# Four-bit feed-forward with its norm inside the rounding stage, and a sign layer joined with its norm

## The chip, the cores and the metric

The kernel runs on one core of a Trainium2 chip. The metric is the device time of one execution in microseconds (us). The engines are TensorE (PE, matmuls; PEld its weight loads), VectorE (DVE), ScalarE (ACT), GpSimd (POOL) and SyncE (SP, which issues DMAs here). Each works through its own instructions in order and waits at semaphores for the others. Data lies in SBUF or in PSUM, the memory that TensorE writes.

## The reference, cut to what matters

A stream of 8 sequences of 512 tokens with 128 channels passes eight layers, each added to the stream after a layer norm (state space, four-bit feed-forward, linear attention, four-bit feed-forward, forgetting attention, sign layer, rotary attention, sign layer). The two layers that the change rewrites:

```python
def _layernorm(x, axis=-1, eps=1e-05):
    m = jnp.mean(x, axis=axis, keepdims=True)
    v = jnp.var(x, axis=axis, keepdims=True)
    return (x - m) / jnp.sqrt(v + eps)
def fp4_quant_dequant(x):             # BLOCK = 16 along the last dimension
    xb = x.reshape(shape[:-1] + (shape[-1] // BLOCK, BLOCK))
    scale = jnp.max(jnp.abs(xb), axis=-1, keepdims=True) / 6.0
    scale = jnp.maximum(scale, jnp.float32(1e-12))
    xn = xb / scale
    idx = jnp.searchsorted(_MID, jnp.abs(xn))
    q = _GRID[idx] * jnp.sign(xn) * scale      # grid 0, .5, 1, 1.5, 2, 3, 4, 6
    return q.reshape(shape)
def _L0_ffn_ref(x, w_gate, w_up, w_down):      # 128 -> 352 -> 128
    gate = fp4_linear(x, w_gate)               # both sides are rounded first
    y = fp4_linear(x, w_up)
    h = jax.nn.silu(gate) * y
    return fp4_linear(h, w_down)
def _L1_ffn_ref(x, weight):
    return jnp.einsum('bsi,oi->bso', x, jnp.sign(weight))
...
x = x + _L0_ffn_ref(_layernorm(x, axis=-1), ...)
```

## The kernel before, in words

The stream `X` and its norm `XN` stay in SBUF as 128 channels x 8 sequences x 512 tokens in f32. The program is a row of stages. A `Stage` (L55) ends with a barrier of all engines, so nothing of one stage runs beside the next. Its tiles carry its name as a prefix in the trace (`ln_`, `fx_`, `fh_`, `sf_`, `fu_`). An f32 matmul shows as two PE instructions, a transpose as one.

`layernorm_stage` (L133) writes `XN`, a sequence at a time: TensorE subtracts the mean by a matmul with `center`, VectorE copies the result out (L208), ScalarE squares it, TensorE sums the squares of four sequences into one PSUM tile, ScalarE takes Ln and Exp, VectorE refines the inverse root by one Newton step of three operations (`refine`, L212 to L216), TensorE spreads it (L169) and VectorE multiplies (L221).

`ffn0_stages` (L647) has two stages. `fx` rounds the normed tokens, one sequence at a time. ScalarE copies, TensorE transposes to 128 tokens x 128 channels (L676), VectorE takes each block's largest magnitude, makes `scale` and a slightly larger `above`, divides, and finds a rounding constant `mag` for each value from its exponent bits by two operations. GpSimd adds and subtracts `mag`, which rounds. VectorE multiplies by `scale` (L720), and TensorE turns it back (L682). `fh` works on 32 tiles of 128 tokens. For each, TensorE multiplies by the gate and up weights (128x352, L767, L768), ScalarE takes Tanh, VectorE forms `h` in SBUF and rounds it as in `fx`, two tiles in step. GpSimd adds, subtracts and multiplies by `scale` (L861 to L868), TensorE transposes (L775), ScalarE copies to `HT`, and once per sequence (four tiles) TensorE multiplies by the down weights into `y` (L782) and VectorE adds that to `X` (L843). VectorE's nine operations stand in loops over tile pairs, of which each ends before the next:

```python
for t, done in both:
    dve.wait_ge(s.amax, done)
    dve.tensor_scalar(scale[t][:, :], amax[t][:, :], 1.0 / 6.0, 2e-12, ALU.mult, ALU.max).then_inc(s.scale, 1)
for t, done in both:
    dve.tensor_scalar(above[t][:, :], amax[t][:, :], ABOVE / 6.0, ABOVE * 2e-12, ALU.mult, ALU.max).then_inc(s.above, 1)
```

`ffn1_stage` (L964) multiplies `XN` by the signs of the weights (L976) and VectorE adds to `X` (L983). After the last one a stage of its own stores `X` by four DMAs (L248).

`forget_units` (L1059) is one pipeline over 64 units (a sequence and two heads). In its turns `i` from -8 a unit `a = i + 8` is projected (`kvps`, L1224), filtered by six VectorE operations in `KV` (L1425, `tap`), passed through Tanh back into `kvps` (L1304), and multiplied into keys and values (L1452, L1453). The projection of a unit waits for the values of the one before:

```python
pe.wait_ge(s.sk, a)
pe.wait_ge(s.sv, a)
```

The scores start at `i = 0`, so in the first turns only these steps run. `nps`, `sps` and `P13` serve the scores and are idle until then.

## Time and profile before

| what | value |
|---|---|
| median of 3 runs (lowest, highest) | 2548.9 us (2546.92, 2555.17) |
| profiled execution, its own time | 2549.09 us |
| its span | 2547.3 us |
| busy, PE / DVE / ACT / POOL | 1965.4 / 1695.2 / 1371.0 / 966.0 us |

The profile is one execution. The span runs from the first instruction to the last. Busy shares are means over stages that have different limits, so the profile is read stage by stage: the timeline gives where a stage begins and ends, and within it the engine that never idles, or the chain of waits, sets its length. The forgetting attention takes the largest part of the span (L1059 and on), and little of it is touched.

### The profile page before, as it was taken

What the parts mean: (1) busy time and instruction counts of PE and PEld (TensorE: products, weight loads), DVE (VectorE), ACT (ScalarE), POOL (GpSimd) and SP (SyncE); (2) the same over time, 40 slices, a digit from 0 to 9 for tenths busy, and PEclk for the clock granted to TensorE, in tenths of its full rate; (3) what the DMA queues carried; (4) which work ended last, traced back from release to release, by engine and by line L of the source; (5) the groups of instructions that cost most, each with busy time, mean ns of one, the idle gap of its engine ahead of it and who ended that gap; (6) DMA issues with size and microseconds to landing.
All of it is one profiled execution on the core that took longest, in us unless ns stands there. A gap on an engine that the chain in (4) does not pass through costs nothing. (4 is left out here: it accounts for less than half of the span.)

```text
span 2547.3 us, 38051 instructions
## 1 busy us (share of the span) xinstructions
PE 1965.4 (77%) x11759; PEld 874.1 (34%) x11759; DVE 1695.2 (67%) x2691; ACT 1371.0 (54%) x2091; POOL 966.0 (38%) x810
## 2 busy tenths in 40 slices
PE   5368876276782664589999999999999867589885
PEld 2123321133451331244444444444444313222221
DVE  5979985588435884577888888788886436611113
ACT  3356652122341222467777777777775513398882
POOL 0256661357003570144455555455555403600000
PEclk9779997578895886899999999999999968799998
DMA  2000000000000001011111111121111100411110
GB/s 84 0 13 0 0 0 0 0 0 0 0 0 0 1 0 48 22 42 53 56 56 60 54 54 54 60 64 59 54 63 61 40 15 25 100 43 44 49 37 33
DMA packets 66118, 85.81 MB, mean 34 GB/s; under 512 B 13344, under 2 KB 37216, under 8 KB 65888
## 3 DMA queue, kind: packets, MB, share of 16 engines
q1 hardware_dynamic: 60944, 81.37, 10.4%
q10 hardware_dynamic: 5040, 2.72, 0.4%
q8 instruction: 76, 1.25, 0.2%
q14 instruction: 58, 0.48, 0.1%
HBM read 72.12 MB, written 11.93 MB: 33 GB/s over the span
## 5 line engine op out<-in xcount | busy, mean ns | idle before, releaser
L1425 DVE SCALAR_TENSOR_TENSOR fu_kv<-fu_ps_kv,fa_vec,fu_kv 128x511 f32<-128x511 f32 (+2 forms) x384 | 265.4, 740 | 22.6 <-ACT fu_kv L1342 21.7
L1782 ACT ACTIVATE rt_p<-rt_ps_s 128x1024 f32<-128x1024 f32 x256 | 242.7, 1026 | 43.7 <-PE rt_ps_s L1719 43.0
L1497 POOL TENSOR_TENSOR fu_p<-fu_p 128x768 f32<-128x768 f32 x64 | 116.9, 1826 | 262.6 <-PE fu_ps_n L1196 258.2
L1166 PE MATMUL fu_ps_s<-fu_qn,fu_kn 64*128 64x512 f32 (+3 forms) x1024 | 191.2, 471 | 7.5 <-ACT fu_p L1329 5.6
L600 POOL TENSOR_TENSOR scan_hC<-scan_h,scan_c 128x1024 f32<-128x1024 f32 x64 | 150.8, 2356 | 83.0 <-DVE scan_h L580 83.0
L1224 PE MATMUL fu_ps_kv<-w_XN,fa_wp 128*128 128x512 f32 x256 | 138.3, 666 | 42.0 <-DVE fu_vs L1453 26.7
L1196 PE MATMUL fu_ps_n<-fu_p,fu_vt 128*64 128x512 f32 (+3 forms) x1024 | 166.0, 445 | 0.0
L525 PE MATMUL scan_ps_y<-scan_hC,w_ident 128*128 128x512 f32 x256 | 130.4, 633 | 41.0 <-POOL scan_hC L600 24.3
L580 DVE TENSOR_TENSOR_SCAN scan_h<-scan_dA,scan_ps_b 128x1024 f32<-128x1024 f32 x64 | 146.4, 2287 | 2.2
L1508 POOL TENSOR_TENSOR fu_num<-fu_num,fu_sg 128x512 f32<-128x512 f32 x64 | 81.4, 1272 | 168.9 <-DVE fu_sg L1458 168.9
L1730 PE MATMUL rt_ps_o<-rt_p,rt_va 128*32 128x512 f32 x1024 | 137.9, 611 | 4.5 <-POOL rt_va L1707 3.5
L1166 PEld LDWEIGHTS fu_ps_s<-fu_qn,fu_kn 64*128 64x128 f32 x1024 | 82.8, 185 | 126.7 <-ACT fu_p L1346 52.1
L1719 PE MATMUL rt_ps_s<-ra_stackq,ra_stackk 48*128 48x512 bf16 x512 | 92.7, 390 | 41.5 <-ACT rt_p L1782 22.6
L1342 ACT ACTIVATE fu_kv<-fu_ps_kv,fa_vec 128x512 f32<-128x512 f32 x128 | 86.6, 687 | 68.2 <-PE fu_ps_kv L1224 63.9
L1398 DVE SCALAR_TENSOR_TENSOR fu_og<-fu_num,fu_ow,fu_ro 128x512 f32<-128x512 f32 x64 | 81.0, 1266 | 57.6 <-POOL fu_num L1508 49.8
L1492 POOL TENSOR_TENSOR fu_kn<-fu_ks,fu_rb 128x512 f32<-128x512 f32 x64 | 98.7, 1543 | 40.2 <-DMA fu_rb<-rms_rows 40.1
L1402 DVE TENSOR_REDUCE fu_nm<-fu_ps_m 128x2 f32<-128x1024 f32 x64 | 78.0, 1219 | 45.2 <-PE fu_ps_m L1189 45.2
L561 ACT ACTIVATE scan_c<-scan_ps_c 128x1024 f32<-128x1024 f32 x64 | 65.5, 1024 | 75.6 <-POOL scan_hC L600 46.5
L796 ACT ACTIVATE fh_th<-fh_ps_g 128x352 f32<-128x352 f32 x64 | 29.7, 464 | 134.7 <-PE fh_ps_u L768 134.7
L1458 DVE SCALAR_TENSOR_TENSOR fu_sg<-fu_sg,fu_ps_s 128x512 f32<-128x512 f32 x64 | 44.0, 688 | 80.3 <-ACT fu_sg L1318 80.0
L1487 POOL TENSOR_TENSOR fu_sqk<-fu_ks 128x512 f32<-128x512 f32 x64 | 66.6, 1040 | 78.9 <-DVE fu_ks L1452 78.5
L1707 POOL COPY rt_va<-ra_v 128x128 f32 x32 | 8.1, 296 | 232.7 <-PE rt_ps_o L1730 232.3
(311 smaller groups left out, 5115.8 us busy)
## 6 DMA issues: line engine op xcount, KB each, us to landing
fu_rb<-rms_rows SPq DMA_DIRECT2D x256, 128.0 KB, 2.9
fu_ro<-rms_rows SPq DMA_DIRECT2D x128, 128.0 KB, 3.0
ra_stackq<-rope_parts SPq DMA_DIRECT2D x168, 32.0 KB
ra_stackk<-rope_parts SPq DMA_DIRECT2D x168, 32.0 KB
rope_parts<-rp_q SPq DMA_DIRECT2D x24, 128.0 KB, 2.0
rope_parts<-rp_k SPq DMA_DIRECT2D x24, 128.0 KB, 2.0
rms_rows<-fu_r SPq DMA_DIRECT2D x14, 192.0 KB, 2.1
w_X<-in_xT SPq DMA_DIRECT2D x4, 512.0 KB
```

The source lines that it names most:

```text
L525: i = pe.matmul(yps[:, :], w.ident[:, :], hC[p % (BEHIND + 2)][:, j, :], start=(p == 0 and j == 0), stop=(p == PAIRS - 1 and j == 1))
L580: dve.tensor_tensor_scan(flat[0], flat[1], flat[2], 0.0, ALU.mult, ALU.add).then_inc(s.scan, 1)
L600: pool.tensor_tensor(hC[p % (BEHIND + 2)][:, :, :], hst[p % 2][:, :, :], csb[p % 2][:, :, :], ALU.mult).then_inc(s.hC, 1)
L1166: pe.matmul(sps[:, h, at:at + T - t * P], k[head(h), t * P:(t + 1) * P], q[head(h), t * P:T], start=(at == 0), stop=False)
L1196: m = pe.matmul(nps[head(h), t * P:T], VT[b % VR][:, t, head(h)], p[:, h, :], start=(t == 0), stop=(t == 2))
L1224: pe.matmul(kvps[:, j, :], wp[:, g, 1 + j, :], XN[:, n, :], start=True, stop=True).then_inc(s.kvp, 1)
L1425: dve.scalar_tensor_tensor(acc, kvps[:, k, 0:T - j], vec[:, a % GA, at:at + 1], acc, ALU.mult, ALU.add).then_inc(done, 1)
L1492: pool.tensor_tensor(KN[u % 3][:, :], K[u % KR][:, :], RB[:, 1, :], ALU.mult).then_inc(s.kn, 1)
L1497: pool.tensor_tensor(tail, tail, P13[:, :, 0:3 * P], ALU.add).then_inc(s.d1, 1)
L1719: m = pe.matmul(sps[i][:, e, :], stack[1][rows, 2 * q4 + i, t * P:(t + 1) * P], stack[0][rows, 2 * q4 + i, :], start=True, stop=True)
L1730: m = pe.matmul(ops[q4 % 2][32 * j:32 * j + 32, :], va[:, t, 4 * q4 + j, :], pr[k % 2][j // 2][:, j % 2, :], start=(t == 0), stop=(t == NT ...
L1782: act.activation(pr[k % 2][i][:, :, :], sps[i][:, :, :], ACT.Exp, scale=DH_B ** -0.5).then_inc(s.exp, 1)
```

## The change: what it does

The stages `ln2`, `ln4`, `ln6` and `ln8` are gone.

**fx.** It works on pairs of sequences (four pairs, tiles of 128 tokens x 1024). TensorE makes the centred tokens at once in token rows (`center(k)`, with a piece of `X` as the stationary side) into a ring of three PSUM tiles. ScalarE squares with a sum per token (8 instructions of 128x128 a pair), and Ln and Exp of 128x8 give the rough inverse root. VectorE refines it on 128x8 tiles. It takes block maxima of the centred values, and one multiplication in place in PSUM applies norm and scale together. ScalarE takes absolute values times 2^22 (`size`), VectorE forms `tot` = max(`size`, ROUND) + value, GpSimd forms `mag` = max(`size`, ROUND), `q` = `tot` - `mag`, and multiplies by `above`. The multiplication that VectorE did at L720 is thus GpSimd's.

**fh.** The tiles run singly, with no loop instructions. `h` and the scaled value stay in PSUM (`ups`, three tiles). ScalarE takes the absolute values. GpSimd has the same three operations as in `fx`. TensorE does gate of tile `j+1`, up of `j`, then the transposes of `j-3` and, every fourth tile, the down product.

**sf.** `norm_ffn1_stage` multiplies `X` by `mix`, the product of centring and signs, while the norm is still being made. ScalarE copies the product out, VectorE scales it, GpSimd adds it to `X`, and in the last stage SP stores each pair as it is ready.

**fu.** Units 1, 3 and 5 are projected into `nps` and half of `sps` and filtered in `P13`. The wait of units 1 to 6 is one unit looser (`emptied`), and ScalarE takes Tanh later within the first turns.

The weights' dequantization is divided by ABOVE, in operations that were there as copies. The core of the diff (indentation halved):

```diff
+STEP = 2.0 ** 22
+ROUND = 1.5 * STEP
 ABOVE = 1.0 + 2.0 ** -21
...
-def ffn0_stages(nc, w, X, XN):
...
+def ffn0_stages(nc, w, X):
...
+      cps = [st.ps(f"c{k}", [P, NB, FQ]) for k in range(RING)]
...
+          def center(k):
+            pe.wait_ge(s.tot, max(k - RING + 1, 0))
...
+              m = pe.matmul(cps[k % RING][:, t * XB:(t + 1) * XB, :].rearrange("p a q -> p (a q)"), X[:, n, at:at + P], w.center[:, :], start=True, stop=True)
...
+          center(0)
+          center(1)
+          for k in range(PAIRS):
+            if k + 2 < PAIRS:
+              center(k + 2)
+            back(k)
...
+              act.wait_ge(s.sq, max(TOK * k + t - 1, 0))
+              tile = cps[k % RING][:, t * XB:(t + 1) * XB, :].rearrange("p a q -> p (a q)")
+              act.activation(squares[t % 2][:, :], tile, ACT.Square, accum_out=ssq[:, k, t:t + 1]).then_inc(s.sq, 1)
+            act.wait_ge(s.sq, TOK * (k + 1))
...
+            act.activation(size[k % 2][:, :, :], cps[k % RING][:, :, :], ACT.Abs, scale=STEP).then_inc(s.size, 1)
...
+          moments(0)
+          moments(1)
+          for k in range(PAIRS):
+            sizes(k)
+            if k + 2 < PAIRS:
+              moments(k + 2)
+            if k:
+              out(k - 1)
+          out(PAIRS - 1)
...
-              dve.tensor_scalar(above[h][:, :], amax[h][:, :], ABOVE / 6.0, ABOVE * 1e-12, ALU.mult, ALU.max).then_inc(s.above, 1)
...
-              dve.tensor_scalar(mag[h][:, :, :].bitcast(I32), xn[h][:, :, :].bitcast(I32), EXP_MASK, None, ALU.bitwise_and).then_inc(s.exp, 1)
...
-              dve.tensor_scalar(mag[h][:, :, :], mag[h][:, :, :], 1.0, ROUND, ALU.max, ALU.mult).then_inc(s.mag, 1)
...
-              dve.tensor_tensor(xq[1 - h][:, :, :], q[1 - h][:, :, :], widen(scale[1 - h][:, :], FQ), ALU.mult).then_inc(s.xq, 1)
...
+            dve.tensor_reduce(amax[:, k, :], cps[k % RING][:, :, :], AX_X, ALU.max, apply_absolute_value=True).then_inc(s.amax, 1)
...
+            dve.tensor_scalar(var[:, k, :], ssq[:, k, :], 1.0 / D, LN_EPS, ALU.mult, ALU.add).then_inc(s.var, 1)
...
+            dve.scalar_tensor_tensor(v2[:, k, :], v1[:, k, :], -0.5, rough[:, k, :], ALU.mult, ALU.mult).then_inc(s.v2, 1)
...
+            dve.tensor_tensor(tokens(normed[:, k, :]), tokens(amax[:, k, :]), r, ALU.mult).then_inc(s.normed, 1)
...
+            dve.tensor_scalar(above[:, k, :], normed[:, k, :], ABOVE / 6.0, ABOVE * 1e-12, ALU.mult, ALU.max).then_inc(s.above, 1)
...
+            dve.reciprocal(inv[:, k, :], above[:, k, :]).then_inc(s.inv, 1)
...
+            dve.tensor_tensor(tokens(both[:, k, :]), tokens(inv[:, k, :]), r, ALU.mult).then_inc(s.both, 1)
...
+            dve.tensor_tensor(xn, xn, widen(both[:, k, :], FQ), ALU.mult).then_inc(s.xn, 1)
...
+            dve.scalar_tensor_tensor(tot[k % 2][:, :, :], size[k % 2][:, :, :], ROUND, cps[k % RING][:, :, :], ALU.max, ALU.add).then_inc(s.tot, 1)
...
+          for k in range(PAIRS):
+            codes(k)
+            if k + 1 < PAIRS:
+              maxima(k + 1)
+              roots(k + 1)
+            total(k)
...
+            pool.tensor_scalar(mag[k % 2][:, :, :], size[k % 2][:, :, :], ROUND, None, ALU.max).then_inc(s.mag, 1)
...
+            pool.wait_ge(s.tot, k + 1)
...
+            pool.tensor_tensor(q[k % 2][:, :, :], tot[k % 2][:, :, :], mag[k % 2][:, :, :], ALU.subtract).then_inc(s.q, 1)
...
+            pool.tensor_tensor(xq[k % 2][:, :, :], q[k % 2][:, :, :], widen(above[:, k, :], FQ), ALU.mult).then_inc(s.xq, 1)
...
+          def gate(j):
+            pe.wait_ge(s.gt, max(j - 1, 0))
+            pe.matmul(gps[j % 2][:, :], tokens(j), w.gate[:, :], start=True, stop=True).then_inc(s.g, 1)
+
+          def up(j):
+            pe.wait_ge(s.tot, max(j - 2, 0))
+            pe.matmul(ups[j % 3][:, :, :].rearrange(flat), tokens(j), w.up[:, :], start=True, stop=True).then_inc(s.u, 1)
...
+              pe.wait_ge(s.ht, 2 * (j + 1))
...
+          gate(0)
+          for j in range(G + LAG):
+            if real(j + 1):
+              gate(j + 1)
+            if real(j):
+              up(j)
+            if real(j - LAG):
+              end(j - LAG)
...
+          for j in range(G + LAG):
+            if real(j):
+              act.wait_ge(s.g, j + 1)
...
+              act.activation(th[j % NT][:, :, :].rearrange(flat), gps[j % 2][:, :], ACT.Tanh, scale=0.5).then_inc(s.th, 1)
+            k = j - 1
+            if real(k):
+              act.wait_ge(s.xn, k + 1)
...
+              act.activation(size[k % 2][:, :, :], ups[k % 3][:, :, :], ACT.Abs, scale=STEP).then_inc(s.size, 1)
+            k = j - LAG
...
+              act.wait_ge(s.t, k + 1)
...
+              act.activation(HT[m % 2][:, 0:2, t * P:(t + 1) * P], tps[k % 2][:, 0:2, :], ACT.Copy).then_inc(s.ht, 1)
...
-              dve.tensor_scalar(scale[t][:, :], amax[t][:, :], 1.0 / 6.0, 2e-12, ALU.mult, ALU.max).then_inc(s.scale, 1)
...
-              dve.tensor_scalar(mag[t][:, :, :].bitcast(I32), xn[t][:, :, :].bitcast(I32), EXP_MASK, None, ALU.bitwise_and).then_inc(s.exp, 1)
...
-              dve.tensor_scalar(mag[t][:, :, :], mag[t][:, :, :], 1.0, ROUND, ALU.max, ALU.mult).then_inc(s.mag, 1)
...
+            dve.wait_ge(s.th, j + 1)
+            dve.scalar_tensor_tensor(gt[j % 2][:, :, :].rearrange(flat), th[j % NT][:, :, :].rearrange(flat), 1.0, gps[j % 2][:, :], ALU.add, ALU.mult).then_inc(s.gt, 1)
+            dve.wait_ge(s.gt, j + 1)
+            dve.wait_ge(s.u, j + 1)
+            dve.tensor_tensor(h, gt[j % 2][:, :, :].rearrange(flat), h, ALU.mult).then_inc(s.h, 1)
...
+            dve.wait_ge(s.size, j + 1)
+            dve.wait_ge(s.q, max(j - 1, 0))
+            dve.scalar_tensor_tensor(tot[j % 2][:, :, :], size[j % 2][:, :, :], ROUND, ups[j % 3][:, :, :], ALU.max, ALU.add).then_inc(s.tot, 1)
...
+            dve.tensor_scalar(above[r][:, :], amax[r][:, :], ABOVE / 6.0, ABOVE * 2e-12, ALU.mult, ALU.max).then_inc(s.above, 1)
...
+            dve.tensor_tensor(ups[j % 3][:, :, :], ups[j % 3][:, :, :], widen(inv[r][:, :], FQ), ALU.mult).then_inc(s.xn, 1)
+
+          for j in range(G + 1):
+            if real(j):
+              product(j)
+            if real(j - 1):
+              total(j - 1)
+            if real(j):
+              scaled(j)
+            m, t = divmod(j - NT, NT)
+            if t == NT - 1 and m >= 0:
               dve.wait_ge(s.y, m + 1)
               dve.tensor_tensor(X[:, m, :], X[:, m, :], yps[:, :], ALU.add).then_inc(s.x, 1)
...
+            pool.tensor_scalar(mag[j % 2][:, :, :], size[j % 2][:, :, :], ROUND, None, ALU.max).then_inc(s.mag, 1)
...
+def norm_ffn1_stage(nc, w, X, out=None):
...
+          pe.wait_ge(s.sq, max(n - 1, 0))
+          pe.matmul(cps[n % 2][:, :], w.center[:, :], X[:, n, :], start=True, stop=True).then_inc(s.cent, 1)
...
+          pe.wait_ge(s.kept, max(n - 1, 0))
+          pe.matmul(cps[n % 2][:, :], mix[:, :], X[:, n, :], start=True, stop=True).then_inc(s.y, 1)
+
+        pe.matmul(vps[0][:, 0:P], w.center[:, :], w.signT[:, :], start=True, stop=True).then_inc(s.mixp, 1)
...
+        for n in range(B):
+          signed(n)
+          if n == 1 or n == HALF + 1:
+            widen(n // HALF)
...
+          act.activation(ys[:, n, :], cps[n % 2][:, :], ACT.Copy).then_inc(s.kept, 1)
...
+        keep(0)
+        keep(1)
+        root(1)
+        for n in range(2, B):
+          keep(n)
...
+          dve.tensor_tensor(ys[:, n, :], ys[:, n, :], rps[n % HALF][:, :], ALU.mult).then_inc(s.scaled, 1)
+
+        dve.wait_ge(s.mixp, 1)
+        dve.tensor_copy(mix[:, :], vps[0][:, 0:P]).then_inc(s.mix, 1)
...
+          pool.wait_ge(s.y, n + 1)
+          pool.tensor_tensor(X[:, n, :], X[:, n, :], ys[:, n, :], ALU.add).then_inc(s.x, 1)
...
+          for b in range(0, B, 2):
+            sp.wait_ge(s.x, b + 2)
+            sp.dma_start(out[:, b:b + 2, :], X[:, b:b + 2, :]).then_inc(s.put, 16)
...
+    def second(a):
+
+      return a % 2 == 1 and a < AHEAD - 2
+
+    def projected(a, j):
+
+      return ((nps[:, :], sps[:, 1, :])[j]) if second(a) else kvps[:, j, :]
+
+    def taken(a):
+
+      return P13 if second(a) else KV
+
+    def emptied(a):
+
+      return max(a - 1, 0) if a < AHEAD - 1 else a
...
+            pe.wait_ge(s.sk, emptied(a))
...
+              pe.matmul(projected(a, j), wp[:, g, 1 + j, :], XN[:, n, :], start=True, stop=True).then_inc(s.kvp, 1)
...
+          if not real(m):
+            queries()
+            transposed()
+            tanhs()
+            gates()
...
+      lambda: None, lambda: ffn0_stages(nc, w, X),
...
+      lambda: None, lambda: norm_ffn1_stage(nc, w, X),
...
+      lambda: None, lambda: norm_ffn1_stage(nc, w, X, out),
...
+    if hi < len(steps):
+      store_output(nc, X, out)
```

VectorE in `fh`. Before, it takes a pair of tiles in step; after, one tile, with `tot` of the tile before between its product and its maxima:

```order
L815 SCALAR_TENSOR_TENSOR fh_gt<-fh_th,fh_ps_g 128x352 x2
L818 TENSOR_TENSOR fh_h<-fh_gt,fh_ps_u 128x352 x2
L821 TENSOR_REDUCE fh_amax<-fh_h 128x22 x2
L824 TENSOR_SCALAR fh_scale<-fh_amax 128x22 x2
L826 TENSOR_SCALAR fh_above<-fh_amax 128x22 x2
L829 RECIPROCAL fh_inv<-fh_above 128x22 x2
L832 TENSOR_TENSOR fh_xn<-fh_h,fh_inv 128x352 x2
L835 TENSOR_SCALAR fh_mag<-fh_xn 128x352 x2
L838 TENSOR_SCALAR fh_mag<-fh_mag 128x352 x2
```

```order
L880 SCALAR_TENSOR_TENSOR fh_gt<-fh_th,fh_ps_g 128x352
L883 TENSOR_TENSOR fh_ps_u<-fh_gt,fh_ps_u 128x352
L888 SCALAR_TENSOR_TENSOR fh_tot<-fh_size,fh_ps_u 128x352
L893 TENSOR_REDUCE fh_amax<-fh_ps_u 128x22
L896 TENSOR_SCALAR fh_above<-fh_amax 128x22
L898 RECIPROCAL fh_inv<-fh_above 128x22
L900 TENSOR_TENSOR fh_ps_u<-fh_ps_u,fh_inv 128x352
```

Nine operations a tile became seven, and each now stands right behind the one whose result it needs, but for `tot`.

TensorE in `fh`, at the end of a sequence, before and after (`fh_ps_y` is the down product):

```order
L767 MATMUL fh_ps_g<-w_gate,fh_xc 128x352
L768 MATMUL fh_ps_u<-w_up,fh_xc 128x352
L775 MATMUL fh_ps_t<-w_ident,fh_hq 128x128 x2
L775 MATMUL fh_ps_t<-w_ident,fh_hq 96x128
L782 MATMUL fh_ps_y<-fh_ht,w_down 128x512 x3
```

```order
L823 MATMUL fh_ps_g<-w_gate,ffn_xq 128x352
L827 MATMUL fh_ps_u<-w_up,ffn_xq 128x352
L835 MATMUL fh_ps_t<-w_ident,fh_hq 128x128 x2
L835 MATMUL fh_ps_t<-w_ident,fh_hq 96x128
L842 MATMUL fh_ps_y<-fh_ht,w_down 128x512 x3
L823 MATMUL fh_ps_g<-w_gate,ffn_xq 128x352
L827 MATMUL fh_ps_u<-w_up,ffn_xq 128x352
```

The sequence of kinds is the same, but the gate ahead of the down product now belongs to tile `j+1`, the up to `j` and the transposes to `j-3` instead of `j-4`. The up product behind it is the one that VectorE needs next.

TensorE in the first turns of `fu`, before and after, for unit 3:

```order
L1224 MATMUL fu_ps_kv<-w_XN,fa_wp 128x512 x2
L1250 MATMUL fu_ps_ss<-fu_sqq,w_selq 32x512
L1251 MATMUL fu_ps_ss<-fu_sqk,w_selk 32x512
L1263 MATMUL fu_ps_s<-w_XN,fa_wp 128x512
L1280 MATMUL fu_ps_m<-w_ident,fu_vs 128x128 x4
```

```order
L1404 MATMUL fu_ps_n<-w_XN,fa_wp 128x512
L1404 MATMUL fu_ps_s<-w_XN,fa_wp 128x512
L1430 MATMUL fu_ps_ss<-fu_sqq,w_selq 32x512
L1431 MATMUL fu_ps_ss<-fu_sqk,w_selk 32x512
L1443 MATMUL fu_ps_s<-w_XN,fa_wp 128x512
L1460 MATMUL fu_ps_m<-w_ident,fu_vs 128x128 x4
```

The order stands; the place that the projection is written to, and with it what it waits for, moved.

## Rows read from the trace of the kernel before

**Rows 1.** Busy time by stretch: us, each engine's busy time, granted clock, DMA share, GB/s.
```profile
429.90:512.82 82.92, 32.08 (x112) 16.21 (x112) 42.78 (x86) 17.54 (x30) 22.68 (x16) 0.56 0.00 0
512.82:643.71 130.89, 93.48 (x272) 49.72 (x272) 108.72 (x296) 36.93 (x114) 82.00 (x96) 0.84 0.00 0
751.62:833.14 81.52, 30.15 (x112) 15.62 (x112) 42.79 (x86) 17.55 (x29) 22.68 (x16) 0.60 0.00 0
833.14:963.79 130.65, 91.22 (x272) 48.22 (x272) 109.24 (x296) 36.94 (x114) 82.01 (x96) 0.85 0.00 0
1005.05:1054.24 49.19, 28.13 (x62) 9.56 (x63) 27.20 (x41) 20.34 (x30) 4.82 (x5) 0.81 0.00 1
2060.96:2103.36 42.40, 27.39 (x64) 8.90 (x65) 20.09 (x30) 8.51 (x14) 0.00 (x0) 0.72 0.00 0
2502.43:2547.30 44.87, 22.03 (x64) 7.25 (x64) 20.09 (x30) 8.51 (x13) 0.00 (x0) 0.83 0.12 47
```

**Rows 2.** Timeline of DVE in `fh`: start us, us, instruction, [idle before].
```profile
520.99 0.30 DVE L824 TENSOR_SCALAR fh_scale<-fh_amax 128x22 f32<-128x22 f32 x2
...
544.58 0.68 DVE L843 TENSOR_TENSOR w_X<-w_X,fh_ps_y 128x512 f32 x1
...
546.90 0.93 DVE L821 TENSOR_REDUCE fh_amax<-fh_h 128x22 f32<-128x352 f32 x2
547.76 1.14 DVE L824 TENSOR_SCALAR fh_scale<-fh_amax 128x22 f32<-128x22 f32 x2
...
630.98 0.68 DVE L843 TENSOR_TENSOR w_X<-w_X,fh_ps_y 128x512 f32 x1
```

**Rows 3.** Timeline of POOL in `fh`.
```profile
546.29 1.83 POOL L864 TENSOR_TENSOR fh_q<-fh_q,fh_mag 128x352 f32<-128x352 f32 x2
548.08 1.53 POOL L868 TENSOR_TENSOR fh_hq<-fh_q,fh_scale 128x352 f32<-128x352 f32 x2
```

**Rows 4.** Timeline of PE: transposes at half clock, the down product, f32 matmuls.
```profile
454.66 1.97 PE L676 MATMUL fx_ps_t<-w_ident,fx_xc 128*128 128x128 f32 x8 [3.98 <-ACT fx_xc L692]
...
553.27 2.84 PE L782 MATMUL fh_ps_y<-fh_ht,w_down 128*128 128x512 f32 x6 [0.63 <-ACT fh_ht L802]
555.95 0.76 PE L767 MATMUL fh_ps_g<-w_gate,fh_xc 128*128 128x352 f32 x2
556.55 0.75 PE L768 MATMUL fh_ps_u<-w_up,fh_xc 128*128 128x352 f32 x2
...
680.46 1.05 PE L902 MATMUL la_ps_v<-w_vo,la_xc 128*128 128x128 f32 x8
```

**Rows 5.** Groups of instructions by line and form: busy us, mean ns, idle before.
```profile
L936 ACT ACTIVATE la_at<-la_ps_a 128x128 f32<-128x128 f32 x8 | 2.2, 278 | 0.0
L588 DVE TENSOR_TENSOR scan_ps_b<-ssm_dx,scan_ps_b 128x1024 f32<-128x1024 f32 x64 | 77.4, 1209 | 9.3 <-PE scan_ps_b L533 9.3
L600 POOL TENSOR_TENSOR scan_hC<-scan_h,scan_c 128x1024 f32<-128x1024 f32 x64 | 150.8, 2356 | 83.0 <-DVE scan_h L580 83.0
L1478 POOL TENSOR_SCALAR fu_ow<-fa_vec 128x8 f32<-128x8 f32 x1 | 0.2, 238 | 0.1
L1701 POOL MEMSET rt_va<- 128x2048 f32 x1 | 1.8, 1805 | 3.6 <-POOLq L71 3.6
L1508 POOL TENSOR_TENSOR fu_num<-fu_num,fu_sg 128x512 f32<-128x512 f32 x64 | 81.4, 1272 | 168.9 <-DVE fu_sg L1458 168.9
L212 DVE SCALAR_TENSOR_TENSOR ln_v<-ln_ps_v,w_consts,ln_rstd 128x512 f32<-128x512 f32 x16 | 11.9, 746 | 11.0 <-ACT ln_rstd L194 11.0
L214 DVE SCALAR_TENSOR_TENSOR ln_v<-ln_v,ln_rstd 128x512 f32<-128x512 f32 x16 | 11.1, 692 | 0.5
```

**Rows 6.** Timeline of DVE and ACT in `fu`, turn of unit 4.
```profile
1048.34 3.38 DVE L1425 SCALAR_TENSOR_TENSOR fu_kv<-fu_ps_kv,fa_vec,fu_kv 128x511 f32<-128x511 f32 x5 [0.61 <-ACT fu_kv L1342]
1051.75 1.03 ACT L1304 ACTIVATE fu_ps_kv<-fu_kv 128x1024 f32<-128x1024 f32 x1 [3.44 <-DVE fu_kv L1425]
```

**Rows 7.** Timeline at the end: the last norm's first multiplications, and the store.
```profile
2517.09 2.47 DVE L221 TENSOR_TENSOR w_XN<-w_XN,ln_ps_b 128x512 f32<-128x512 f32 x4
2539.43 2.92 SPq L248 DMA_DIRECT2D out_dram<-w_X  x4
```

More of the change, by code:

```diff
@@ new lines, in sizes, with out @@
+                    def sizes(k):
+                        act.wait_ge(s.xn, k + 1)
+                        act.wait_ge(s.mag, max(k - 1, 0))
+                        act.wait_ge(s.tot, max(k - 1, 0))
+                        act.activation(size[k % 2][:, :, :], cps[k % RING][:, :, :], ACT.Abs, scale=STEP).then_inc(s.size, 1)
+                    def out(k):
+                        for j in range(2):
+                            act.wait_ge(s.back, 2 * k + j + 1)
+                            act.activation(XQ[:, 2 * k + j, :], qps[j][:, :], ACT.Copy).then_inc(s.out, 1)
@@ L745, in ffn0_stages @@
-            amax, scale, above, inv = ([st.sb(f"{n}{k}", [P, FB]) for k in range(NT)] for n in ("amax", "scale", "above", "inv"))
-            hh, xn, mag, q, hq = ([st.sb(f"{n}{k}", [P, FB, FQ]) for k in range(NT)] for n in ("h", "xn", "mag", "q", "hq"))
-            HT = st.sb("ht", [P, KF, T])
-            s = st.sems("xc gu th gt h amax scale above inv xn exp mag add q hq t ht y x")
-            flat = "p a q -> p (a q)"
-            def tiles(n, last, tile, end):
-                for t in range(NT):
-                    if n is not None:
-                        tile(n, t)
-                    if last is not None:
-                        end(last, t)
+            th, hq = ([st.sb(f"{n}{k}", [P, FB, FQ]) for k in range(NT)] for n in ("th", "hq"))
@@ L1367, in _ @@
                         tanhs()
+                        transposed()
                     else:
```

380 lines of the change are left out of this document (211 added, 169 removed).

## The prediction, made before the changed kernel ran

> **What bounds the kernel now.** I read the table of stretches first. It shows two norm-and-`fx` stretches of 82.9 and 81.5 us in which no engine is busy for more than 43, and two `fh` stretches of 130.9 and 130.7, where VectorE is busy 108.7, TensorE 93.5 and GpSimd 82.0 [rows 1]. The first are chains: an operation waits for the one before it, sequence by sequence. In `fh` VectorE sets the length: its adds to `X` stand 86.40 us apart over six sequences [rows 2], 14.40 for four tiles, 3.60 a tile; eight such periods are 115.2, and 15.7 fill and drain. In that timeline the pair of `scale` operations takes 0.30 with GpSimd idle and 1.14 while GpSimd's subtraction runs, ending with it at about 548.1 [rows 2, 3]. So this form of VectorE (one SBUF tile in and out, 22 elements) stands still while GpSimd works; the wide ones keep their time. The last two stretches are norm and sign layer (42.4 and 44.9, with the store in the second), and the first turns of `fu`: 49.2 us for five units [rows 1].
>
> The profile's own time is 2549.09, its span 2547.3, the median 2548.9. The sum is made against 2549 without correction.
>
> **Norm and `fx`.** Gone are the norm stage, its passes of 512 and the turn to token rows. New is a chain over four pairs. First pair: centring, 8 matmuls, half by L902's 1.05 at full clock for four (2.1) and half by half clock (the old transposes, 8 in 1.97 at the 1.2 GHz level, are one pass, a matmul two: 4.2), taken 4.0 [rows 4]; squares 8 x 0.278 = 2.2 [rows 5], the sum per token not shown by any row (at nothing 2.2, at twice 4.5; I take 2.6, near the row); maxima and root 2.1; the small products up to `both` 1.25; the multiplication 1.22 (L588's 1.209) [rows 5]; Abs 1.05 (as Tanh over 1024, 1.03) [rows 6]; `tot` 1.22; hops 0.4. That is 14.0.
>
> Then the period. After `tot(k)` GpSimd's `q` takes 2.36 (L600) [rows 5], and `above(k+1)` is the form that stands still: 2.6 until it is through. Reciprocal 0.56, `both` 0.25 and the multiplication bring 4.75, maxima and root of the pair after it 7.6, `tot` 8.8. Two such periods and a third without maxima (7.05) end `tot` of the last pair at 38.7. Behind it: `q` 2.36, the product with `above` 2.1, turning back 2.2 (rows 4's transposes), the copy 0.6: 46. With 0.8 for the stage's change it is 46.8, against 82.9 and 81.5: **-36.1 and -34.7**. GpSimd's max over 1024 has no row: 0.24 by eight elements, 2.36 by a two-input operation, and a memset of 2048 takes 1.81 [rows 5]; I take 1.1. It lies beside Abs-to-`tot` up to 1.2, so only its upper end costs (1.2 a pair). Ends: 38 (nothing held, full clock) and 55 (half clock throughout, squares doubled, that max) a stage.
>
> **`fh`.** Each tile loses `scale`, two passes for `mag` and half of the pairing, and gains `tot`. VectorE's order is product(j), total(j-1), reduce, `above`, reciprocal, multiplication. Durations by the old paces: `gt` 0.55 with its hop, `h` 0.43, `tot` 0.43, reduce 0.51 and a hop (a lone one 0.51, paced 0.43) [rows 2]. At 1.96 `above` is ready, but GpSimd's `q(j-1)`, freed by `tot(j-1)` at about 1.55, takes 0.93 (1.83 for two) [rows 3] and holds it to 2.48; then 0.18 + 0.27 + 0.43 (+0.04) end the tile at **3.40**. Not held it is 2.93. GpSimd has 0.93, 0.77 and the max (0.1 to 0.93, taken 0.45): 2.15, not the bound. ScalarE has Tanh, Abs and two copies, 1.6.
>
> Every fourth tile more comes: the add to `X` at 0.43 beyond what its shadow gives (0.68 alone [rows 2], paced less), and a stall. ScalarE's copies of `ht(j-3)` are queued behind Abs(j-1), and this waits for the multiplication of j-1, at the end of the tile before. So `ht` is done 1.15 into the tile, and only then does TensorE start `y`. From its start to the end of the next up product the trace has 553.27 to 557.30, 4.03 us [rows 4]; so up(j+1) lands at 5.2, where VectorE wants it at 3.40 + 0.55 = 3.95. Stall 1.3, behind which total, reduce and the whole next tile queue. Sum: fill 5.9, 31 x 3.40 = 105.4, 7 x 1.76 = 12.3, tail 8.7 (q, hq, transposes, copies, `y`, the last add), stage change 0.8: 133, and 1 for stretches at half clock: 134. Against 130.8: **+3.2 each, +6.4**. The gain of the dropped operations goes to `above`'s hold and the new stall. Ends: 119 (neither) and 158 (half clock throughout: four tiles' PE work 4 x 3.3 + 5.2 = 18.5, x 8, and fill). The clock granted in `fh` was 0.84, in the stretch of norm and `fx` 0.56 [rows 1]; TensorE has the same work, so I keep it.
>
> On GpSimd the "GPSIMD Engine Reference" of the Trainium skill (section "Specifications") says that its SBUF interfaces are shared with VectorE, with contention for a 2-port mode or two SBUF inputs. The held `scale` in rows 2 agrees with the first half; the second would add the small root products of `fx`, which is rival 4.
>
> **`fu`, first turns.** A unit takes 49.19/5 = 9.84, which is the sum of projection, taps (3.38 for five and a sixth before) and Tanh in a row, with 3.44 of idle before each Tanh [rows 1, 6]. With a second set of tiles, projection and Tanh lie beside the other unit's taps, and the period falls to taps 4.1 + keys and values 1.3 + part of Tanh's 1.03: 6.4 to 7, the first about 8 for the clock. Five intervals: about 35 for 49: **-15** (ends -8 and -20). The 64 turns after it keep their work.
>
> **Norm and sign layer.** The product no longer waits for the norm. Path: the first centring, square, root 15 us to the first add; then GpSimd's eight adds. Each is 1.27 (L1508) [rows 5], with one delayed behind VectorE's second root, ending about 25.7; leaving and change 1.8 + 0.75: 28.3 less the overlap of the first, 28.3 against 42.40 [rows 1]: **-14.1**. The last norm's multiplications (2.47 for four [rows 7]) go too, and the store lies beside the adds except for its last DMA. The four DMAs landed 7.9 us after the first started (2539.43 to 2547.3) [rows 7]; for the last alone I take 3.9 (ends 2 and 7.9). 26.2 + 3.9 = 30.1 against 44.87: **-14.8**.
>
> Sum: -36.1 - 34.7 + 6.4 - 15 - 14.1 - 14.8 = -108.3; 2549.1 - 108.3 = **2441**. For the likeliest case alone the open prices (max, square's sum, last DMA, fill) give 2425 to 2456.
>
> **Rivals.**
> 1. *`above` isn't held, or the up product isn't late.* With tiles running singly, `q` might fall beside other operations. Then `fh` runs at 2.93 + little, some 119 a stage: -15 each against the likeliest with `fx` a little shorter, 2413. For it: the hold depends on half a microsecond of phase. Against it: `tot(j-1)` frees `q` right ahead of `above` in VectorE's own order.
> 2. *TensorE at half clock bounds `fh`.* With its longer waits for `ht` it idles more, and half of the groups of four run at 1.2 GHz: half of 18.5 - 15.4 = 3.1 x 8, 12 a stage: 2465. For it: 0.56 in the stretch where it worked least. Against it: 0.84 in the old `fh` with the same work [rows 1].
> 3. *PSUM costs.* All of `h`, maxima, multiplication and `tot` read PSUM now. Rows 5 have 0.746 from PSUM beside 0.692 from SBUF, the same 512: 0.054 x 4 x 64 = 14: 2455. Against it: L588 does 1024 wholly in PSUM in 1.209, no slower than the pace of SBUF. "VectorE: DVE Perf Modes" of the Trainium skill (the section on the trn2 errata) gives 120 fixed cycles at 0.96 GHz for a PSUM source and 58 for SBUF, an estimate of 0.065 us each, 16.5 in all; its author rules offer a copy to SBUF where many operations follow, the opposite of this change. The 0.054 of rows 5 agrees.
> 4. *Small root products held too.* In `fx`, v2 or `both` also stand behind `q` or the product with `above`: 1.3 a pair, 6 pairs: +8: 2449, inside the likeliest's range.
> 5. *The change does not reach `fu`.* If keys and values (on VectorE or GpSimd) and not the tiles are what a unit waits for, its 15 stay: 2456.
> 6. *Slower: GpSimd's max bounds `fh`.* It has 0.93 + 0.77 besides. From 3.40 + 108/64 = 5.1 a tile on the whole gain is gone, so the max over 352 would have to take 3.4; at 3.5 the time is 2555. Eight elements take 0.238 and a memset of 2048 1.805 [rows 5], which speaks strongly against it.
>
> **How the numbers follow.** Likeliest 0.52, rival 1 0.17, rival 2 0.15, rival 3 0.07, rival 4 0.05, rival 5 0.03, rival 6 0.01. The range 2405 to 2475 takes rivals 1 to 5 with their own uncertainty, and leaves out half clock throughout (2489) and every term at its low end (2385). 0.3% of this time is 7.6 us, about what a measurement tells from no change: faster 0.98, same 0.01, slower 0.01.
>
> **What the profile after would show.** `fx` with its norm 46 us; its `above` far over 0.2 and ending with GpSimd's `q`. In `fh` adds to `X` 15.4 apart, `above` some 0.6 to 0.7, and once in four tiles VectorE idle 1.3 before `h`, freed by the up product, with `y` just before it on TensorE; adds 12 to 13 apart would be rival 1, with idle before every `h` and a clock near 0.6 rival 2. GpSimd's max near 0.45 and 1.1. In `fu` the first scores 15 us sooner after the stage's start. The sign layers end with GpSimd's adds 1.27 apart. Under 2405 the hold and the stall in `fh` are both wrong, over 2475 it is the clock or an unpriced operation.

## The result, and the profile after

| | before | after |
|---|---|---|
| median (lowest, highest), us | 2547.91 (2546.31, 2555.17) | 2472.73 (2463.62, 2476.36) |
| ratio, 95% interval | | 0.9696 (0.9668 to 0.9725) |
| profiled span, us | 2547.3 | 2474.6 |

The change makes the kernel 75 us faster; forecast were 108. The time lies inside the forecast's range of 2405 to 2475, close to its upper end, and 32 us above the forecast of 2441. The stretches of [rows 1], in the profile after (first two norm with `fx` and `fh`, then the same again, the first units of `fu`, the two sign layers; columns as there). The stretch of `fu` is cut to the length that it had before, and now holds the keys of six units instead of five:

```profile
429.61:476.07 46.46, 18.06 (x96) 16.53 (x96) 25.73 (x44) 20.23 (x85) 28.15 (x12) 0.61 0.00 1
476.07:622.44 146.37, 98.23 (x272) 51.85 (x273) 112.85 (x232) 42.44 (x130) 89.60 (x96) 0.82 0.00 1
730.64:775.90 45.26, 16.69 (x96) 15.07 (x96) 25.72 (x44) 20.23 (x85) 28.15 (x12) 0.64 0.00 1
775.90:922.52 146.62, 100.16 (x272) 52.66 (x272) 112.75 (x232) 42.50 (x130) 89.60 (x96) 0.80 0.00 1
963.82:1013.00 49.18, 32.03 (x84) 12.02 (x84) 32.13 (x49) 28.54 (x45) 6.25 (x6) 0.88 0.04 14
2008.58:2038.54 29.96, 21.47 (x66) 6.97 (x67) 10.56 (x15) 13.14 (x22) 10.46 (x8) 0.91 0.00 1
2440.66:2474.60 33.94, 22.63 (x66) 7.56 (x66) 10.56 (x15) 13.03 (x21) 10.47 (x8) 0.85 0.15 62
```

| step | forecast | measured | off by |
|---|---|---|---|
| norm and `fx`, twice | -36.1, -34.7 | -36.5, -36.3 | -2.0 |
| `fh`, twice | +3.2, +3.2 | +15.5, +16.0 | +25.1 |
| `fu` | -15 | -11.2 (1059.2 to 1048.0) | +3.8 |
| sign layers | -14.1, -14.8 | -12.4, -10.9 | +5.6 |
| the norm behind the first sign layer (`ln7`) | 0 | +2.5 (22.8 to 25.3) | +2.5 |
| span | -108.3 | -72.7 | +35.6 |

Seven tenths of the miss are in `fh`. VectorE lost 64 instructions there (296 to 232), but its busy time rose from 108.7 to 112.9: some of what is left takes longer than it did. Its idle time rose too, from 22.2 to 33.5. The timeline of one group of four tiles shows both, where [rows 2, 3] showed them before:

```profile
529.75 0.51 DVE L880 SCALAR_TENSOR_TENSOR fh_gt<-fh_th,fh_ps_g 128x352 f32<-128x352 f32 x1
530.24 0.38 ACT L872 ACTIVATE fh_ht<-fh_ps_t 128x256 f32<-128x256 f32 x1
530.43 1.09 POOL L921 TENSOR_SCALAR fh_mag<-fh_size 128x352 f32<-128x352 f32 x1 [0.64 <-ACT fh_size L866]
530.74 0.51 DVE L888 SCALAR_TENSOR_TENSOR fh_tot<-fh_size,fh_ps_u 128x352 f32<-128x352 f32 x1
531.60 0.93 POOL L925 TENSOR_TENSOR fh_q<-fh_tot,fh_mag 128x352 f32<-128x352 f32 x1
531.72 0.84 DVE L896 TENSOR_SCALAR fh_above<-fh_amax 128x22 f32<-128x22 f32 x1
...
533.36 0.51 DVE L880 SCALAR_TENSOR_TENSOR fh_gt<-fh_th,fh_ps_g 128x352 f32<-128x352 f32 x1
534.43 4.80 PE L842 MATMUL fh_ps_y<-fh_ht,w_down 128*128 128x512 f32 x6 [0.76 <-ACT fh_ht L873]
536.96 0.51 DVE L880 SCALAR_TENSOR_TENSOR fh_gt<-fh_th,fh_ps_g 128x352 f32<-128x352 f32 x1
539.07 0.76 PE L823 MATMUL fh_ps_g<-w_gate,ffn_xq 128*128 128x352 f32 x2
539.66 0.75 PE L827 MATMUL fh_ps_u<-w_up,ffn_xq 128*128 128x352 f32 x2
540.52 0.53 DVE L883 TENSOR_TENSOR fh_ps_u<-fh_gt,fh_ps_u 128x352 f32<-128x352 f32 x1 [3.05 <-PE fh_ps_u L827]
```

`gt` of the next tile comes 3.61 later (529.75, 533.36), not 3.40. GpSimd's max takes 1.09 (taken: 0.45) and ends at 531.52, after `tot` at 531.25; so the subtraction starts late, and `above`, 22 elements, ends with it at 532.5. And the down product runs 4.80 us, most of it at the 1.2 GHz level (granted clock 0.59 over its length; 2.84 us in [rows 4]); VectorE waits 3.05 for the up product behind it.

### The profile page after: what moved, and what is told of

Same layout as the page of the kernel before. It is cut to its first block and busy times, and to the rows that moved or that the text cites. A ratio compares the mean times of both kernels' runs of the same rounds, so it can differ in the third digit from the quotient of the medians.

```text
span 2474.6 us, 37339 instructions
## 1 busy us (share of the span) xinstructions
PE 1943.5 (79%) x11731; PEld 880.3 (36%) x11731; DVE 1648.7 (67%) x2449; ACT 1395.7 (56%) x2254; POOL 1013.6 (41%) x818
## 5 line engine op out<-in xcount | busy, mean ns | idle before, releaser
L1618 DVE SCALAR_TENSOR_TENSOR fu_kv<-fu_ps_kv,fa_vec,fu_kv 128x511 f32<-128x511 f32 x366 | 252.6, 739 | 7.3 <-ACT fu_kv L1526 6.4
L1404 PE MATMUL fu_ps_kv<-w_XN,fa_wp 128*128 128x512 f32 x244 | 125.1, 636 | 18.1 <-DVE fu_cr L1583 15.4
L866 ACT ACTIVATE fh_size<-fh_ps_u 128x352 f32<-128x352 f32 x64 | 29.7, 464 | 151.9 <-DVE fh_ps_u L900 151.9
L562 ACT ACTIVATE scan_c<-scan_ps_c 128x1024 f32<-128x1024 f32 x64 | 65.5, 1024 | 75.2 <-POOL scan_hC L601 46.4
L823 PE MATMUL fh_ps_g<-w_gate,ffn_xq 128*128 128x352 f32 x128 | 61.9, 573 | 56.8 <-DVE fh_gt L880 53.7
```

Source lines behind the costliest of these rows:

```text
L1404: pe.matmul(projected(a, j), wp[:, g, 1 + j, :], XN[:, n, :], start=True, stop=True).then_inc(s.kvp, 1)
L1618: dve.scalar_tensor_tensor(acc, projected(a, k)[:, 0:T - j], vec[:, a % GA, at:at + 1], acc, ALU.mult, ALU.add).then_inc(done, 1)
```

## The experiments

Stage lengths from the beginning of the first to the end of the last instruction, from each kernel's profile (the stages are separated by barriers, so each can be read by itself):

| kernel | median us | ratio to before, 95% | `fx` | `fh` | `fu` | `sf` |
|---|---|---|---|---|---|---|
| before | 2547.9 | | | 130.0, 129.8 | 1059.2 | |
| changed | 2472.7 | 0.9696 (0.9668 to 0.9725) | 45.6, 44.4 | 145.5, 145.7 | 1048.0 | 28.9, 29.9 |
| a_fh_old | 2432.7 | 0.9558 (0.9542 to 0.9574) | 45.4, 44.4 | 127.8, 129.2 | 1041.2 | 28.9, 27.2 |
| a_above_first | 2430.1 | 0.9543 (0.9527 to 0.9559) | 45.6, 44.4 | 124.6, 123.2 | 1046.1 | 29.7, 29.9 |
| a_y_parts | 2439.5 | 0.9581 (0.9562 to 0.9599) | 45.5, 44.4 | 128.8, 128.8 | 1046.3 | 29.8, 29.9 |
| a_mag_vector | 2474.3 | 0.9717 (0.9701 to 0.9733) | 45.6, 44.4 | 145.7, 146.3 | 1050.0 | 29.8, 29.9 |
| b_both | 2406.9 | 0.9437 (0.9402 to 0.9472) | 45.3, 44.3 | 111.6, 112.1 | 1046.7 | 28.9, 30.8 |
| b_ht_fx | 2424.6 | 0.9512 (0.9493 to 0.9532) | 48.7, 47.0 | 117.6, 117.0 | 1046.2 | 29.7, 29.7 |
| b_all | 2407.8 | 0.9465 (0.9437 to 0.9493) | 48.7, 47.0 | 111.8, 110.0 | 1042.6 | 29.5, 30.5 |
| b_fu_old | 2487.5 | 0.9768 (0.9747 to 0.9789) | 45.3, 44.4 | 145.2, 145.6 | 1060.7 | 27.3, 29.9 |
| c_both | 2404.8 | 0.9435 (0.9416 to 0.9455) | 45.3, 44.3 | 111.5, 112.0 | 1047.0 | 28.9, 29.9 |
| c_small | 2407.7 | 0.9458 (0.9441 to 0.9474) | 48.1, 45.5 | 111.8, 111.3 | 1045.9 | 27.3, 27.1 |

**a_fh_old.** The whole old stage `fh` behind the new `fx`, of which the first lines that differ are:

```diff
-            ups = [st.ps(f"u{k}", [P, FB, FQ]) for k in range(3)]
+            ups = [st.ps(f"u{k}", [P, FF]) for k in range(2)]
...
```

> The changed kernel with the tile stage fh of the kernel before; the joined fx, fu and the sign layers stay as changed. Theory (fh by itself became slower, by 15.5 us in each of its two stages: 130.9 to 146.4): the two fh stages return to 130.5 to 131.5, the rest doesn't move, and the time is 2472.7 - 31 = 2442 (2438 to 2446). Rival (fh is slower because of what fx hands over, its clock or its data): fh stays above 138 and the time above 2456.

The theory holds for the stage: 127.8 and 129.2, 17 us less each. The time, 2432.7, is 9 below what was expected; 7 of them stand in `fu`, which is the same in both kernels and which measures 1041 to 1050 in the ten profiles that have the new one. The rewriting of `fh` by itself is a loss.

**a_above_first.** VectorE's order in `fh`; `largest` has the maxima and `above`, which `scaled` had before the reciprocal and the multiplication:

```diff
                             product(j)
+                            largest(j)
                         if real(j - 1):
                             total(j - 1)
                         if real(j):
                             scaled(j)
```

> One edit in fh: VectorE takes the maxima and `above` of tile j ahead of `tot` of tile j-1, so GpSimd's subtraction starts after `above` and cannot hold it. Theory (the hold costs 0.45 to 0.66 in each tile): `above` 0.15 to 0.2 instead of 0.74 on the mean, ordinary tiles 2.95 apart instead of 3.40 to 3.61; the stall at the up product stays 2.5 to 3, a group of four tiles 15.6 to 16.2 instead of 17.36, fh 134 to 138, the time 2472.7 - 20 = 2453 (2447 to 2459). Rival 1 (TensorE's work and its clock set the group): what `above` gives, the stall takes, fh 144 to 147, the time within 5 of 2472.7. Rival 2 (GpSimd holds whatever comes next, now the reciprocal): as rival 1 but with the reciprocal at 0.8.

More than the theory had: 124.6 and 123.2, and 2430.1 in all. The tiles are as it said; the stall, which it kept at 2.5 to 3, fell to 1.76. A group in the timeline of this kernel:

```profile
526.85 2.85 PE L842 MATMUL fh_ps_y<-fh_ht,w_down 128*128 128x512 f32 x6 [1.68 <-ACT fh_ht L873]
527.44 0.18 DVE L896 TENSOR_SCALAR fh_above<-fh_amax 128x22 f32<-128x22 f32 x1
527.53 0.52 DVE L888 SCALAR_TENSOR_TENSOR fh_tot<-fh_size,fh_ps_u 128x352 f32<-128x352 f32 x1
528.18 0.93 POOL L929 TENSOR_TENSOR fh_q<-fh_tot,fh_mag 128x352 f32<-128x352 f32 x1
528.28 0.53 DVE L903 TENSOR_TENSOR fh_ps_u<-fh_ps_u,fh_inv 128x352 f32<-128x352 f32 x1
530.98 0.53 DVE L883 TENSOR_TENSOR fh_ps_u<-fh_gt,fh_ps_u 128x352 f32<-128x352 f32 x1 [1.76 <-PE fh_ps_u L827]
```

`above` takes 0.18, tiles are 2.95 apart, and beside the subtraction runs the multiplication in PSUM at its usual 0.53. The reciprocal takes 0.28 and isn't held in the place of `above`: rival 2 falls. The groups are 14.10, all alike: the stall is 1.76 each time, because the down product always takes 2.85. The windows row of `fh` here and in b_both shows TensorE's clock back near its upper level with the same matmuls:

```profile
476.00:598.00 122.00, 79.39 (x270) 44.47 (x271) 94.42 (x231) 42.53 (x129) 88.47 (x96) 0.95 0.00 1
```
```profile
476.00:580.00 104.00, 75.79 (x263) 40.37 (x262) 94.58 (x231) 39.95 (x126) 88.45 (x96) 0.97 0.00 1
```

So the half clock (0.82 in the changed kernel) was not a cause of its own: an edit of VectorE's order alone takes it away. Slower tiles by themselves don't bring it, for in a_y_parts, below, they are 3.60 and the clock is 0.92; what lets it fall was not isolated. In the changed kernel it made a stall of 1.1 (down product at 2.85, two groups of seven in the first stage) one of 2.2 to 3.05 (five of seven).

**a_y_parts.** The down product in three pieces (`part(m, c)` is chunk `c`; `end` keeps only the transposes):

```diff
                         if real(j - LAG):
                             end(j - LAG)
+                        m, c = divmod(j - LAG - NT, NT)
+                        if m >= 0 and c < KF:
+                            part(m, c)
```

> One edit in fh: the down product's three chunks are issued by TensorE one in each of the three tiles after the last transposes of a sequence, each behind the next gate and up product, and VectorE adds to X three tiles later. Theory (the stall of 1.1 to 3.05 us, once in four tiles, is the up product queued behind the whole down product): no wait of VectorE for the up product over 0.3, groups 14.6 to 15.2, fh 124 to 129 with a tail longer by 1, the time 2472.7 - 36 = 2437 (2430 to 2446). Rival (TensorE at its half clock is what bounds the group): waits of 0.5 to 1 spread over all tiles, fh 138 to 144, the time 2458 to 2470.

The wait for the up product is gone (1.41 at the first tile and, in the second stage, one of 0.40), and the stage falls by 17, the theory's price at its upper end (128.8 for 124 to 129). The groups are 14.8 (3.40, 3.61, 3.60, 3.60 and 0.60 for the add to X): the hold alone remains, and its mean is larger than in the changed kernel (0.78 for 0.74):

```profile
L901 DVE TENSOR_SCALAR fh_above<-fh_amax 128x22 f32<-128x22 f32 x32 | 25.0, 782 | 1.1
```

The clock was 0.92, and TensorE bounded nothing: the rival falls.

**a_mag_vector.** GpSimd's max in `fh` on VectorE:

```diff
+                        dve.tensor_scalar(mag[j % 2][:, :, :], size[j % 2][:, :, :], ROUND, None, ALU.max).then_inc(s.mag, 1)
-                        pool.tensor_scalar(mag[j % 2][:, :, :], size[j % 2][:, :, :], ROUND, None, ALU.max).then_inc(s.mag, 1)
```

> One edit in fh: GpSimd's max (1.09 us a tile) is done by VectorE, from SBUF to SBUF, right ahead of `tot`. It tells how much of the hold comes from GpSimd's max, which makes its subtraction start later. Theory: VectorE gains an operation of 0.25 a tile (8 us a stage), the subtraction starts with the end of `tot`, `above` takes 0.6 in every tile instead of 0.84 in three of four (5 us a stage back): fh 147 to 151, the time 2474 to 2482. Rival (GpSimd with its 2.8 us a tile and its max paces fh): fh 135 to 140, the time 2447 to 2460.

As the theory has it (stage 145.7 and 146.3, a shade under its range): tiles 3.65, `above` 0.62 on the mean. VectorE's max takes 0.34, not 0.25, and seven down products of fourteen, not ten, run at the low clock. Taking 35 us of work from GpSimd gives nothing: it was never the bound of `fh`.

**b_both** has both edits of a_above_first and a_y_parts, **c_both** is the same kernel again.

> The edits of a_above_first and a_y_parts together, in fh. Theory (hold and stall are separate costs, and TensorE at full clock has 10.6 us of work in four tiles): every tile 2.95, the add to X 0.60 on top once in four, groups 12.4, no wait for the up product, fh 109 to 112, the time 2472.7 - 71 = 2402 (2396 to 2408). Rival (once VectorE is at 2.95, GpSimd with 2.80 a tile or TensorE's clock takes over): groups 13.2 or more, fh 116 to 122, the time 2412 to 2425.

> The kernel of b_both once more, beside the next one on the same chip. fh 111 to 112.5, fx 45.3 and 44.4, the time 2400 to 2410.

As the theory has it: tiles 2.95 throughout, groups 12.4, `fh` 111.6 and 112.1. This version beats both kernels: 0.9437 and 0.9435 of before, against 0.9696. The two edits together give 34 a stage, each alone 17 to 22.

**b_ht_fx.** a_above_first with two more edits: ScalarE's Abs in `fh` moved behind the copies, and the max in `fx` on VectorE.

```diff
-                        k = j - 1
-                        if real(k):
...
-                            act.activation(size[k % 2][:, :, :], ups[k % 3][:, :, :], ACT.Abs, scale=STEP).then_inc(s.size, 1)
                         k = j - LAG
...
+                        k = j - 1
+                        if real(k):
...
+                            act.activation(size[k % 2][:, :, :], ups[k % 3][:, :, :], ACT.Abs, scale=STEP).then_inc(s.size, 1)
...
+                        dve.tensor_scalar(mag[k % 2][:, :, :], size[k % 2][:, :, :], ROUND, None, ALU.max).then_inc(s.mag, 1)
```

> The edit of a_above_first, and two more. In fh ScalarE copies ht(j-3) ahead of Abs(j-1) instead of behind it. Theory (as the prediction has it, the copy is late because it is queued behind Abs, which waits for the multiplication): the down product starts 0.95 earlier, the wait for the up product falls from 1.76 to 0.8, groups from 14.1 to 13.2, fh from 124 to 117.5 (115 to 119). Rival (the copy is late by its transposes): fh within 1.5 of 124. In fx, VectorE takes over GpSimd's max (2.77 us for 1024). Theory (from the second pair on GpSimd's three operations, 7.04 a pair, set the end of fx): GpSimd 4.3 a pair, fx 42 to 43.5 instead of 45.6 and 44.4 (beginning of its first to end of its last instruction). Rival (VectorE's chain sets it, as the prediction had it): fx 45 to 48, longer by what VectorE adds. The time: 2430 - 13 - 4 = 2413 (2408 to 2420).

In `fh` the stall fell from 1.76 to 0.71 in every group, and the stage to 117.6: the copy was late because it stood behind Abs. In `fx` VectorE's chain sets the end, as the rival said, and the first stage is even longer than its range (48.7 and 47.0), which puts the time above what was expected. The trace of b_ht_fx says how:

```profile
444.02 2.34 POOL L788 TENSOR_TENSOR fx_q<-fx_tot,fx_mag 128x1024 f32<-128x1024 f32 x1 [47.47 <-DVE fx_tot L771]
444.05 2.36 DVE L758 TENSOR_SCALAR fx_above<-fx_normed 128x64 f32<-128x64 f32 x1
446.44 1.93 POOL L791 TENSOR_TENSOR fx_xq<-fx_q,fx_above 128x1024 f32<-128x1024 f32 x1
446.45 0.55 DVE L760 RECIPROCAL fx_inv<-fx_above 128x64 f32<-128x64 f32 x1
447.04 1.42 DVE L762 TENSOR_TENSOR fx_both<-fx_inv,fx_rstd 128x64 f32<-128x64 f32 x1
```

and in the changed kernel:

```profile
440.97 2.77 POOL L786 TENSOR_SCALAR fx_mag<-fx_size 128x1024 f32<-128x1024 f32 x1 [45.20 <-ACT fx_size L715]
441.06 0.97 DVE L746 TENSOR_TENSOR fx_v<-fx_var,fx_rough 128x8 f32<-128x8 f32 x1
442.06 0.17 DVE L748 SCALAR_TENSOR_TENSOR fx_v<-fx_v,fx_rough 128x8 f32<-128x8 f32 x1
443.73 0.20 DVE L758 TENSOR_SCALAR fx_above<-fx_normed 128x64 f32<-128x64 f32 x1
443.82 2.34 POOL L790 TENSOR_TENSOR fx_q<-fx_tot,fx_mag 128x1024 f32<-128x1024 f32 x1
443.96 0.55 DVE L760 RECIPROCAL fx_inv<-fx_above 128x64 f32<-128x64 f32 x1
444.55 1.70 DVE L762 TENSOR_TENSOR fx_both<-fx_inv,fx_rstd 128x64 f32<-128x64 f32 x1
```

There `above` starts 0.09 before the subtraction, which the slow max delays, and escapes; `both`, with two SBUF inputs, is held instead (1.70 for 0.22), to the subtraction's end. With the max gone from GpSimd the subtraction starts 0.03 before `above`, and both are held, 2.36 and 1.42. The first pair (from one Abs to the next) takes 9.38 for 7.70: some 0.6 of that is the max that VectorE now does itself, and 1.1 the longer hold. So a lighter GpSimd makes `fx` 3 us longer, in part by the work that moved and in part by the hold.

**b_all.** b_both, the max of `fx` on VectorE, and the sign layer's adds on VectorE:

```diff
-                    pool.tensor_tensor(X[:, n, :], X[:, n, :], ys[:, n, :], ALU.add).then_inc(s.x, 1)
+                    dve.tensor_tensor(X[:, n, :], X[:, n, :], ys[:, n, :], ALU.add).then_inc(s.x, 1)
```

> The edits of b_both, the max of fx on VectorE as in b_ht_fx, and in the sign layer the eight adds to X on VectorE instead of GpSimd. Theory for the sign layers (GpSimd's eight adds of 1.27 and its hold of 0.95 on the second root set their end): sf 26.5 to 27.5 instead of 28.9 and, with the store behind, 31 to 32 instead of 33.9. Rival (the sign layer is bound by ScalarE's copies and the spreading matmuls): 28.5 or more. The time, by the theories: 2402 - 4 - 4 = 2394 (2388 to 2402).

The sign layers don't gain (29.5 and 30.5; the kernels that leave them as changed scatter from 27.1 to 30.8), so moving GpSimd's adds wins nothing that is seen; which of the rival's two limits holds them is open. `fx` is as in b_ht_fx, 6 us longer in all. The time is that of b_both and misses the theory: the profile has the 6 us back in `fu` (4 less, within its scatter) and in the second `fh`, by 2.

**b_fu_old.** The whole old `forget_units`: units 1, 3 and 5 in the same tiles as the others, the old order of ScalarE's Tanh, and the old waits:

```diff
-                        pe.wait_ge(s.sk, emptied(a))
-                        pe.wait_ge(s.sv, emptied(a))
+                        pe.wait_ge(s.sk, a)
+                        pe.wait_ge(s.sv, a)
```

> The changed kernel with forget_units of the kernel before, all else as changed. Theory (the two sets of tiles in the first turns are worth 14.5 to 15.5 up to the first scores): fu longer by 11 to 16, the time 2484 to 2489. Rival (what is won in the first turns comes back in the turns that follow, which wait for something else): fu longer by under 5, the time under 2479.

`fu` 1060.7 and the time 2487.5, 14.7 more than the changed kernel: the theory. Against the mean of the ten profiles with the new `fu`, 1046.0, the gain is 14.7 (13.2 by the kernel before), so the 11.2 of the first comparison is one sample of a stage that scatters by 9.

**c_small.** In `fx`, the small operations of the next pair (`codes`: normed, above, reciprocal, both) ahead of `tot`:

```diff
                         if k + 1 < PAIRS:
                             maxima(k + 1)
                             roots(k + 1)
+                            codes(k + 1)
                         total(k)
```

> The kernel of b_both, and in fx the small operations of pair k+1 (normed, above, reciprocal, both) stand ahead of `tot` of pair k on VectorE instead of behind it, as in fh. Theory (GpSimd's two-input operations hold every operation of VectorE that takes one or two SBUF tiles and no PSUM tile; behind the maxima of pair k+1 they now meet the product with `above` of pair k-1 and its max): the hold on `both` (1.7 a pair, two pairs) goes, but var or v1 takes 1 to 2 instead, a pair still needs 7.2 to 7.8, and since GpSimd needs 7.04 a pair in any case fx can gain 3.4 at most: fx 43 to 46 against 45.3, the time within 5 of c_both. Rival (the root operations of 128x8 are too short to be held, only those of 128x64 are): 5.6 to 6 a pair on VectorE, GpSimd's 7.04 without a gap, fx 42 to 42.5.

The mechanism is the theory's, its range isn't in the first stage: `fx` gets longer, 48.1 and 45.5 for 45.3 and 44.3, and the time is 2.9 above c_both. The hold on `both` goes and returns on the root, for operations of eight elements: 1.79, to the end of GpSimd's product with `above`, and then 0.97 beside its max:

```profile
449.54 1.95 POOL L797 TENSOR_TENSOR fx_xq<-fx_q,fx_above 128x1024 f32<-128x1024 f32 x1
449.72 1.79 DVE L748 SCALAR_TENSOR_TENSOR fx_v<-fx_v,fx_rough 128x8 f32<-128x8 f32 x1
451.46 2.76 POOL L790 TENSOR_SCALAR fx_mag<-fx_size 128x1024 f32<-128x1024 f32 x1
451.54 0.97 DVE L750 SCALAR_TENSOR_TENSOR fx_rstd<-fx_v,fx_rough 128x8 f32<-128x8 f32 x1
```

## Why the prediction was right in sign and 33 us off

**Norm and `fx`** came out as forecast (46.5 and 45.3 for 46.8), by two errors that cancel, which is luck. `tot` of the last pair ends 34.5 into the stage, not at 38.7, since `above` escaped the hold and the last pair met none. But GpSimd's max takes 2.77, above even the upper end of 2.36 that the rows gave, and so GpSimd, with 7.04 a pair, ends the stage:

```profile
458.17 2.77 POOL L786 TENSOR_SCALAR fx_mag<-fx_size 128x1024 f32<-128x1024 f32 x1 [2.30 <-ACT fx_size L715]
461.02 2.34 POOL L790 TENSOR_TENSOR fx_q<-fx_tot,fx_mag 128x1024 f32<-128x1024 f32 x1
462.91 1.22 DVE L770 SCALAR_TENSOR_TENSOR fx_tot<-fx_size,fx_ps_c 128x1024 f32<-128x1024 f32 x1 [1.09 <-ACT fx_size L715]
463.44 1.93 POOL L793 TENSOR_TENSOR fx_xq<-fx_q,fx_above 128x1024 f32<-128x1024 f32 x1
465.34 2.77 POOL L786 TENSOR_SCALAR fx_mag<-fx_size 128x1024 f32<-128x1024 f32 x1
468.19 2.34 POOL L790 TENSOR_TENSOR fx_q<-fx_tot,fx_mag 128x1024 f32<-128x1024 f32 x1
470.61 1.93 POOL L793 TENSOR_TENSOR fx_xq<-fx_q,fx_above 128x1024 f32<-128x1024 f32 x1
```

Rival 4 was true as a mechanism (`both` 0.96 and the first root product 0.57 on the mean, for 0.22 and 0.17), and hidden in the same way. It is also what the "GPSIMD Engine Reference" of the Trainium skill says in its section "Specifications", of VectorE instructions with two SBUF inputs. The traces agree: `both` takes 1.70 beside the subtraction here, and an operation of eight elements 1.79 in c_small.

**`fh`** is the step that failed, in size: +3.2 a stage were forecast, +15.5 and +16.0 measured, with adds to `X` mostly 17.4 apart and not 15.4. Both its mechanisms were right: the hold of `above` (a_above_first: 2.95 without it, the forecast's 2.93) and the stall of the up product behind `y`, late because of Abs (b_ht_fx). Two terms were mis-sized. The tile, "3.40", is 3.61 in most, since GpSimd's max, taken at 0.45, takes 1.09 and delays the subtraction by 0.2; about 4 us a stage. The stall, "1.3", is 2.25 on the mean of seven (1.09 to 3.05), because the down product before it fell to the 1.2 GHz level in five groups; 6.5 us. The rest is small: the add to `X` costs 0.60 for 0.43 (1 us), and fill and tail are 1 to 2 longer than forecast, with the last `y` at the low clock (5.10). Less the 1 us that was set aside for half clock, that makes 12 to 13 a stage. "TensorE has the same work, so I keep" the clock of 0.84 was the wrong argument: the mean stayed (0.82, 0.80), but the low stretches fell where TensorE was waited for: of the down products ahead of the last in each stage, ten of fourteen ran at the low clock, and two of fourteen before. Rival 2 gave 12 a stage and 2465, near the measured 2472.7, though not as it was put: the groups were not bounded by TensorE's work, only one operation in each was. Rival 1 did not come true in the changed kernel, and its 119 a stage is 7 above the 112 that b_both shows with hold and stall taken away.

One reading went too far. In [rows 2] "the wide ones keep their time" holds for the reduction, but not for the multiplication from SBUF in the same stage, which took 0.83 beside GpSimd's product with `scale` (14 such cases, 0.71 to 0.83) and 0.49 to 0.52 alone:

```profile
542.38 0.83 DVE L832 TENSOR_TENSOR fh_xn<-fh_h,fh_inv 128x352 f32<-128x352 f32 x1
```

It cost the forecast nothing in `fh`, whose wide operations have a tile in PSUM.

**Rival 3, PSUM.** The tile without hold is 2.95, the forecast from the old paces 2.93. The multiplication follows at 0.44 in place in PSUM and at 0.41 from SBUF. By these differences, times 64 tiles, some 1 to 2 of the 14 us are seen (an estimate). The estimate of 16.5 from "VectorE: DVE Perf Modes" of the Trainium skill isn't seen either.

**`fu`** held: keys 7.97, 6.59 and 6.67 apart in the first turns (8 and 6.4 to 7), first scores 75.1 after the stage's start instead of 90.4; the rest is the stage's scatter.

**Sign layers.** GpSimd's adds end the stage and are 1.27 each, but the first starts 17.0 after the stage's start, not 14.9, and the eight take 11.9, not 10.8:

```profile
2018.29 0.75 DVE L1112 SCALAR_TENSOR_TENSOR sf_v<-sf_ps_v,w_consts,sf_rstd 128x512 f32<-128x512 f32 x1 [8.89 <-ACT sf_rstd L1090]
2024.81 1.29 DVE L1121 TENSOR_TENSOR sf_ys<-sf_ys,sf_ps_r 128x512 f32<-128x512 f32 x2 [4.31 <-PE sf_ps_r L1055]
2025.57 3.03 POOL L1138 TENSOR_TENSOR w_X<-w_X,sf_ys 128x512 f32<-128x512 f32 x2 [25.63 <-DVE sf_ys L1121]
2027.51 1.64 DVE L1116 SCALAR_TENSOR_TENSOR sf_fine<-sf_v,sf_rstd 128x512 f32<-128x512 f32 x1
2032.53 4.94 POOL L1138 TENSOR_TENSOR w_X<-w_X,sf_ys 128x512 f32<-128x512 f32 x4 [0.21 <-DVE sf_ys L1121]
```

The refined root is ready at 2020.5, and VectorE waits 4.31 for the spreading matmuls, which stand in TensorE's order behind the second variance and two signed products. `sf_fine` is held by the second add (1.64 for 0.69), which had itself waited for the operation of VectorE ahead of `sf_fine` (two adds in 3.03). That the order costs this was read here and not tried. The store's last piece took 4.0 beyond the stage, as forecast (3.9).

**What was given back.** The norm behind the first sign layer is 2.5 longer. Its instructions are the same, its clock is not (0.84, now 0.77); before and after:

```profile
2103.40:2126.20 22.80, 12.58 (x48) 4.03 (x49) 14.58 (x22) 8.65 (x14) 0.00 (x0) 0.84 0.00 1
```
```profile
2038.50:2063.90 25.40, 15.13 (x48) 5.00 (x49) 14.58 (x22) 8.68 (x14) 0.00 (x0) 0.77 0.00 0
```

TensorE used to work to the end of the sign layer; now the layer ends with adds on GpSimd, in which TensorE is idle (5.0 us up to the norm, 1.6 before), and the norm starts at the lower level. That this idle is the reason was not tested by itself.

## What to carry to other kernels

An operation moved to an idle engine is priced twice: by what it takes there, and by the moment at which it lets the operation behind it start, since that decides which small operation of another engine is held. Where one engine is waited for once in a group, price that wait at both of TensorE's clock levels, and ask what stands ahead of the waited-for instruction in its queue; here two reorderings (a small operation ahead of the one that frees GpSimd, a long matmul cut in three) turned a stage that had become 12% slower into one 14% faster than before.

## What the hardware showed that was not expected

- GpSimd's max with a constant takes 1.086 us for 128x352 and 2.77 for 128x1024, longer than its subtraction of two tiles (0.93 and 2.34). VectorE does the same in 0.34 and 0.69.
- GpSimd's two-input operations and most of VectorE's operations with all tiles in SBUF exclude each other. VectorE's stood still to the end of GpSimd's with 8, 22, 64 and 512 elements, with one input or two. Not held were the reciprocal (0.55 beside the subtraction), the reduction from SBUF in the kernel before (0.51 in each of the 60 that met one), and what has a tile in PSUM (0.53 beside the subtraction). Under GpSimd's one-input max some were held by 0.8 to 0.9 (0.97 for 0.17, 1.07 for 0.20), some by less (0.61 for 0.22) and others not at all (0.17, 0.19); the runs give no rule for which.
- ScalarE's squares of 128x128 with a sum need a second instruction of 0.19 to 0.26 each, but the pairs follow at 0.25: 8 in 2.2, what the forecast had for squares without a sum. No run has them without it.
